# Turning six of twelve probability chunks by DMA, with a single buffer, and moving the row statistics and the normalized rows in a two-layer graph attention kernel

## The reference

```python
# layer 0
scores = where(adj > 0, x @ w0 @ inp.T, -2**32 + 1)
x = layernorm(x + softmax(scores / 0.07, axis=1) @ inp)
# layer 1
Wh = x @ W;  s1 = Wh @ a1;  s2 = Wh @ a2
e = leaky_relu(s1[:, None] + s2[None, :], 0.2)
att = softmax(where(adj > 0, e, -9e15), axis=1)
x = layernorm(x + elu(att @ Wh))
```

## Time and profile before

| what | value |
|---|---|
| median of 3 runs | 1454.98 us |
| the profiled execution's own time | 1453.21 us |
| its span, first to last instruction | 1451.4 us |
| TensorE busy | 1412.1 us, 97% |
| VectorE busy | 1256.5 us, 87% |
| GpSimd busy | 1215.0 us, 84% |
| ScalarE busy | 1070.0 us, 74% |
| packets of the main DMA queue, share of 16 engines | 73.1% |
| granted TensorE clock, mean | 0.989 |

### The profile page before, as it was taken

How to read it: one execution, slowest core, us unless ns; L and a number is a source line. 1 busy time by engine, 2 the same in 40 slices (tenths; PEclk the granted TensorE clock), 3 DMA queues, 4 the chain that set the end, 5 groups by cost and what they waited for, 6 DMA issues and landing times.

```text
span 1451.4 us, 28334 instructions
## 1 busy us (share of the span) xinstructions
PE 1412.1 (97%) x9661; PEld 1010.3 (70%) x9661; DVE 1256.5 (87%) x2129; ACT 1070.0 (74%) x2437; POOL 1215.0 (84%) x904
## 2 busy tenths in 40 slices
PE   8899999999999999999999999979999999999995
PEld 4577777777777777777777777755666666666664
DVE  6999999999999899999999999839898898979794
ACT  6788888888888888888888888868655555545453
POOL 6788888888888888888888878738999999999995
PEclk9999999999999999999999999998999999999998
DMA  8999999999999999999999999663434344434320
GB/s 265 292 270 269 262 265 257 258 275 270 270 267 263 259 264 258 273 271 271 273 258 259 262 255 274 182 138 73 102 66 111 77 102 87 102 71 105 78 58 14
DMA packets 427918, 291.38 MB, mean 201 GB/s; under 512 B 356864, under 2 KB 403200, under 8 KB 427776
## 3 DMA queue, kind: packets, MB, share of 16 engines
q1 hardware_dynamic: 427776, 289.59, 73.1%
HBM read 160.56 MB, written 40.89 MB: 139 GB/s over the span
## 4 chain that ended last, share of the span: by engine, by line
PE 94%; DVE 3%; issue 1%; ACT 1%; POOL 0%; DMA 0%; ACTq 0%; DVEq 0%; SPq 0%; POOLq 0%
PE ps L617 17%; PE ps L703 13%; PE ps L696 12%; PE ps L643 11%; PE ps L619 9%; PE ps L656 8%; PE ps L655 8%; PE ps L654 8%; PE ps L680 6%; PE ps L587 1%; PE ps L714 1%; DVE rows L969 1%; DVE neg_mask L944 1%; PE ps L580 0%; DVE pT_lo L978 0%
## 5 line engine op out<-in xcount | busy, mean ns | idle before, releaser
L826 ACT ACTIVATE rows<-rows,exp_bias 128x512 f32<-128x512 f32 x576 | 416.8, 724 | 57.0 <-DVE exp_bias L1022 57.0
L528 POOL TENSOR_TENSOR p_lo<-p,p_hi 128x1024 fp32r<-128x1024 f32 x180 | 423.7, 2394 | 22.0 <-ACT p_hi L864 11.5
L969 DVE CUSTOM_DVE_ANT_0 rows<-ps,neg_mask 128x1024 f32<-128x1024 f32 x288 | 352.1, 1223 | 80.2 <-PE ps L656 72.8
L1049 DVE SCALAR_TENSOR_TENSOR p<-ps,e_col,edgesT 128x1024 f32<-128x1024 f32 x288 | 349.7, 1275 | 53.3 <-PE ps L673 36.7
L438 POOL TENSOR_SCALAR edges<-neg_mask 128x1536 uint8<-128x1536 bf16 x190 | 307.3, 1618 | 97.0 <-DVE neg_mask L944 85.1
L864 ACT CAST p_hi<-p 128x1024 fp32r<-128x1024 f32 x180 | 185.1, 1047 | 167.0 <-DVE p L1049 164.4
L617 PE MATMUL ps<-vals,pT_hi 128*128 128x256 f16 x1536 | 295.3, 273 | 1.4 <-ACT att L805 0.9
L812 ACT CAST pT_hi<-ps 128x512 f16<-128x512 f32 x384 | 222.7, 580 | 90.6 <-PE ps L643 90.4
L480 POOL TENSOR_TENSOR inp_sb<-rows,inp_sb 128x512 f16<-128x512 f32 x192 | 281.5, 1484 | 9.6 <-ACT inp_sb L820 1.9
L619 PE MATMUL ps<-vals,pT_lo 128*128 128x128 f16 x1536 | 274.6, 219 | 0.0
L978 DVE TENSOR_TENSOR pT_lo<-ps,pT_hi 128x512 f16<-128x512 f32 x384 | 250.8, 683 | 10.6 <-ACT pT_hi L812 10.6
(11 more groups left out here) (111 smaller groups left out, 1855.9 us busy)
## 6 DMA issues: line engine op xcount, KB each, us to landing
adj_sb<-adj SPq DMA_DIRECT2D x192, 768.0 KB, 5.6
edge_rows<-edges SPq DMA_DIRECT2D x192, 192.0 KB, 4.8
xq<-x SPq DMA_DIRECT2D x48, 64.0 KB, 2.9
xr<-x SPq DMA_DIRECT2D x48, 64.0 KB, 5.6
out<-y_w SPq DMA_DIRECT2D x5, 512.0 KB, 3.7
inp_sb<-inp SPq DMA_DIRECT2D x3, 768.0 KB, 8.2
inp_sb<-inp_sb SPq DMA_TRANSPOSE x96, 4.6
edgesT<-edge_rows SPq DMA_TRANSPOSE x48, 5.3
```

Source lines behind the costliest of these rows:

```text
L528: nc.gpsimd.tensor_tensor(p1_lo[:, m % LO_SLOTS, :], p1[:, (NB * g + n) % P_SLOTS, :], p1_hi[:, m % HI_SLOTS, :].bitcast(F32), ALU.subtrac ...
L826: nc.scalar.activation(row_chunk(1 - par, c), row_chunk(1 - par, c), ACT.Exp, bias=exp_bias[:, 1 - par:2 - par], scale=EXP_SCALE, accum_ou ...
L969: nc.vector.tensor_tensor_reduce(row_pair(par, k), scores_pair(k), neg_mask_row[:, 2 * k * CHUNK:2 * (k + 1) * CHUNK], 1.0, -3.0e38, ALU.a ...
L1049: nc.vector.scalar_tensor_tensor(out=p1[:, (NB * g + n) % P_SLOTS, :], in0=ps[:, R_ROW:R_ROW + 2, :].rearrange("p b w -> p (b w)"), scalar ...
```

## The change

Six chunks instead of four go by DMA, so that six are turned by TensorE, and ATT_STEP becomes 11. `movedT` loses its second slot and is filled in two parts of three chunks, each part with a high and a low transpose of 384 KB. A part may be overwritten when the attends of the tile before have read it; the casts and subtractions of a chunk wait for the part it is in.

GpSimd's order is new: the reciprocal root is behind the first low part, the product behind the third, low parts 4 and 5 behind edges 0 and 1. It loses the normalizing and the total.

VectorE takes the row statistics of tile t - 3 at step 2 of lap t, behind the first maximum of the tile, and the normalized rows at step 4. For the last tile it also makes the two additions and the products. The total over x1 becomes eight reductions over 44 tiles in lap 48 and four more one-column products on TensorE.

```diff
-MOVED = 4
+MOVED = 6
+MOVED_PARTS = ((0, 3), (3, 6))
...
-        movedT = inp_space[:, 2 * MW:6 * MW].rearrange("p (s h b m) -> p s h b m", s=2, h=2, m=P)
+        movedT = inp_space[:, 2 * MW:4 * MW].rearrange("p (h b m) -> p h b m", h=2, m=P)
...
+        STATS_STEP, ROWS_STEP, SUMS_STEP = 2, 4, 9
+        TOTALLED, TOTAL_PARTS = NB - 4, 8
...
         def movedT_loads(tile):
-            return 32 * (tile // 2 + 1)
+            return 32 * (tile + 1)
+
+        def moved_part(i):
+            return next(k for k, (a, b) in enumerate(MOVED_PARTS) if a <= i < b)
...  SP
-                    if tile < 2:
-                        sp.wait_ge(vals_lo, MOVED * (tile + 2))
-                    after(sp, pv_done, C * (tile - 1))
-                    sp.dma_start_transpose(movedT[:, par, 0], moved_hi).then_inc(movedT_in[par], 16)
-                    sp.wait_ge(moved_lo_set, MOVED * (tile + 1))
-                    sp.dma_start_transpose(movedT[:, par, 1], moved_lo).then_inc(movedT_in[par], 16)
+                    if tile == 0:
+                        sp.wait_ge(vals_lo, 2 * MOVED)
+                    for k, (a, b) in enumerate(MOVED_PARTS):
+                        after(sp, pv_done, C * (tile - 1) + (C - MOVED) + b if tile >= 1 else 0)
+                        for half, of, ready in ((0, moved_hi, moved_hi_set), (1, moved_lo, moved_lo_set)):
+                            sp.wait_ge(ready, MOVED * tile + b)
+                            sp.dma_start_transpose(movedT[:, half, a * BPC:b * BPC, :], of[:, a * CHUNK:b * CHUNK]
+                                                   ).then_inc(movedT_in[k], 16)
...  GpSimd, one lap
                     make_edges(t, 2)
                 if moved:
                     moved_low(t - 1, 0)
+                if t >= 3:
+                    rstd_of_tile(t - 3)
+                if moved:
                     moved_low(t - 1, 1)
                 if 0 < t < NB:
                     make_edges(t, 3)
...
                 if moved:
                     moved_low(t - 1, 2)
+                if t >= 3:
+                    score_cols(t - 3)
+                if moved:
                     moved_low(t - 1, 3)
                 if ahead:
                     make_edges(t + 1, 0)
...
+                if moved:
+                    moved_low(t - 1, 4)
+                if ahead:
                     make_edges(t + 1, 1)
+                if moved:
+                    moved_low(t - 1, 5)
...
-                if ends_tile(known):
+                if 2 <= t <= NB:
...
-                    pool.wait_ge(ve_set, tile + 1)
-                    nc.gpsimd.tensor_tensor(small[:, 4:5], small[:, 3:4], consts[:, 0:1], ALU.pow).then_inc(rstd_set, 1)
-                    pool.wait_ge(rstd_set, tile + 1)
-                    nc.gpsimd.tensor_scalar(x1_all[:, tile, :], xr[:, par, :], moments[:, 0:1], small[:, 4:5], ALU.subtract,
-                                            ALU.mult).then_inc(x1_set, 1)
-                    score_cols(tile)
...  VectorE
+            def row_statistics(tile):
+                dve.wait_ge(u_set, tile + 1)
+                after(dve, x1_set, tile)
+                nc.vector.bn_stats(stats[:], xr[:, tile % 2, :]).then_inc(stats_set, 1)
+                dve.wait_ge(stats_set, tile + 1)
+                nc.vector.bn_aggr(moments[:], stats[:]).then_inc(moments_set, 1)
+                dve.wait_ge(moments_set, tile + 1)
+                nc.vector.tensor_scalar(small[:, 3:4], moments[:, 1:2], EPS, None, ALU.add).then_inc(ve_set, 1)
+
+            def normalized_rows(tile):
+                dve.wait_ge(rstd_set, tile + 1)
+                nc.vector.tensor_scalar(x1_all[:, tile, :], xr[:, tile % 2, :], moments[:, 0:1], small[:, 4:5], ALU.subtract,
+                                        ALU.mult).then_inc(x1_set, 1)
...
                 for c in range(C):
+                    if c == STATS_STEP and t >= 3:
+                        row_statistics(t - 3)
+                    if c == ROWS_STEP and t >= 3:
+                        normalized_rows(t - 3)
...
+                    if t == NB and 1 <= c <= TOTAL_PARTS:
+                        d = slice((c - 1) * P // TOTAL_PARTS, c * P // TOTAL_PARTS)
+                        dve.wait_ge(x1_set, TOTALLED)
+                        nc.vector.reduce_sum(x1_total[:, d], x1_all[:, 0:TOTALLED, d].rearrange("p n d -> p d n"),
+                                             AX_X).then_inc(total_set, 1)
```

More of the change, by code:

```diff
@@ L225, in build @@
         moved_hi_set, moved_lo_set = sem("moved_hi_set"), sem("moved_lo_set")
-        movedT_in = [sem(f"movedT_in{i}") for i in range(2)]
+        movedT_in = [sem(f"movedT_in{i}") for i in range(len(MOVED_PARTS))]
         att_out = sem("att_out")
@@ L478, in moved_low, with rstd_of_tile @@
                 if tile >= 1:
-                    pool.wait_ge(movedT_in[(tile - 1) % 2], movedT_loads(tile - 1))
+                    pool.wait_ge(movedT_in[moved_part(i)], movedT_loads(tile - 1))
                 nc.gpsimd.tensor_tensor(moved_lo[:, i * CHUNK:(i + 1) * CHUNK], row_chunk(tile % 2, i),
                                         moved_hi[:, i * CHUNK:(i + 1) * CHUNK], ALU.subtract).then_inc(moved_lo_set, 1)
+            def rstd_of_tile(tile):
+                pool.wait_ge(ve_set, tile + 1)
+                nc.gpsimd.tensor_tensor(small[:, 4:5], small[:, 3:4], consts[:, 0:1], ALU.pow).then_inc(rstd_set, 1)
             def tile_rstd(t, par, known):
@@ L717, in mean_of_wh @@
             def mean_of_wh():
-                pe.wait_ge(total_set, NB)
-                nc.tensor.matmul(ps[:, SPARE, 0:P], x1_total[:], averager[:], start=True, stop=True).then_inc(mean_turned, 1)
+                pe.wait_ge(total_set, TOTAL_PARTS)
+                nc.tensor.matmul(mean_ps, x1_total[:], averager[:, 0:1], start=True, stop=False)
+                pe.wait_ge(x1_set, NB)
+                for j in range(TOTALLED, NB):
+                    mm = nc.tensor.matmul(mean_ps, x1_all[:, j, :], averager[:, 0:1], start=False, stop=(j == NB - 1))
+                mm.then_inc(mean_turned, 1)
                 pe.wait_ge(mean_repd, 1)
-                nc.tensor.matmul(ps[:, SPARE, P:2 * P], mean_rep[:], w1_c[:, 0:P], start=True, stop=True).then_inc(mean_made, 1)
+                nc.tensor.matmul(ps[:, OUT3, P:2 * P], mean_rep[:], w1_c[:, 0:P], start=True, stop=True).then_inc(mean_made, 1)
             pe.wait_ge(masked, PAIRS * NB)
@@ L830, in tile_steps @@
                         xT_high(t + 1, 1 - par)
-                    if c == 4 and t >= 3:
+                    if c == SUMS_STEP and t >= 3:
                         score_sums(t - 3)
-                    if c == C - 1 and t == NB + 1:
-                        score_sums(t - 2)
                 if t == 0:
@@ L1005, in tile_steps @@
                                                     ALU.mult).then_inc(scaled_set, 1)
[L1006 to L1013, removed]
-                            nc.vector.tensor_scalar(small[:, 3:4], moments[:, 1:2], EPS, None, ALU.add).then_inc(ve_set, 1)
+                        if c == C - 1 and t == NB + 1:
+                            dve.wait_ge(att_out, NB)
+                            dve.wait_ge(xr_in[par], 16 * (t // 2))
+                            nc.vector.tensor_tensor(xr[:, par, :], att[:, 0:P], xr[:, par, :], ALU.add).then_inc(u1_set, 1)
+                            dve.wait_ge(u1_set, NB)
+                            nc.vector.tensor_tensor(xr[:, par, :], att[:, P:2 * P], xr[:, par, :], ALU.add).then_inc(u_set, 1)
                     if c == C - 1 and scores_of(known):
@@ L1025, in _ @@
             tiles(dve, tile_steps)
-            dve.wait_ge(s_set, NB)
+            row_statistics(NB - 1)
+            normalized_rows(NB - 1)
+            dve.wait_ge(x1_set, NB)
+            dve.wait_ge(s_set, NB - 1)
+            for k in range(2):
+                nc.vector.tensor_tensor_reduce(s_prod[:, k, :], x1_all[:, NB - 1, :], wa_rep[:, k, :], 1.0, 0.0, ALU.mult,
+                                               ALU.add, s_cols[:, k, NB - 1:NB]).then_inc(s_last_set, 1)
+            dve.wait_ge(s_last_set, 2)
             nc.vector.reduce_max(s_top[:, 0:1], s_cols[:, 0, :], AX_X).then_inc(s_part, 1)
```

22 lines of the change are left out of this document (10 added, 12 removed).

## The result

The changed kernel takes 1536.99 us (median of 4 runs, 1535.59 to 1538.53), the kernel before 1453.95 beside it (1452.54 to 1455.09): ratio 1.0575, 95% interval 1.0562 to 1.0588. The forecast was 1521 with a range of 1466 to 1562. The profiled execution took 1538.53 with a span of 1536.5, so 85.1 more than the span before.

A forecast was written before the change was run, and what follows sets the result against it. A loop through GpSimd's low parts and VectorE's first maximum and mask quarter 2 was to bound the lap at 20.92 us. 44 laps x 1.57 = 69.1, ends -0.8, on 1453.2 gave 1521 us, range 1466 to 1562.

The forecast's parts named there:

- the way over the last low part: Loop from low 5 through VectorE's first maximum and mask quarter 2 back to low 5: 20.92 us per lap.
- the ends: First laps -1.8 us, lap 47 +1.0, close -1.7, added attends and transposes +1.7: together -0.8 us.
- The closed loop through GpSimd: GpSimd's 16.81 us from edges 2 to low 5 plus VectorE's 4.11 set the lap at 20.92.
- The contention: VectorE's masks lengthen GpSimd's work beside them: 0.59, 0.78 and 0.59, together 1.96 us per lap.
- Almost the same lap, by a second way; ... so this one costs nothing more: VectorE, waiting 2.1 us for rstd in step 4, gives a 20.6 us lap; only the larger loop counts.
- VectorE's account: VectorE's lap: busy time, normalizing at 0.34, waiting for rstd 2.1 and former idling 1.77 sum to 20.6 us.
- The rule weighed in the prediction: VectorE and GpSimd share a port pair as exclusive lock; normalizing could add up to 0.34 us to GpSimd's lap.
- a large wait of L969's first maximum for GpSimd's low part, about 1 us or more per lap: Sign that VectorE's first maximum of a tile is held by the last subtraction, as the GpSimd loop requires.
- The other signs: First scores 20.9 us apart, VectorE waiting 2 for rstd, GpSimd 3 for mask quarter 2, TensorE at nine tenths or less.
- rival 4: The DMA queues bound the lap at 21.1 us, up to 22: 1529 to 1568 us in all; chance 0.10.
- Leaving the share aside: DMA time of 21.1 us per lap was kept only as a rival, since the share counts overlapping packets twice.
- The eight reductions ... stand where VectorE is half idle: Reductions of x1_all in lap 48 on VectorE, given no cost term of their own.

The follow-up runs named there:

- e2: The changed kernel with GpSimd's reciprocal root moved ahead of edges quarter 2: 1489.38 us, ratio 1.0245.
- g2: Five chunks by DMA instead of six, on a version with mask quarter 2 earlier and SP's loads and waits reordered: 1446.09 us, ratio 0.9947.
- e1: The changed kernel with the normalized rows on VectorE at step 7 instead of 4: 1578.94 us, ratio 1.0868.
- f3: As e1, with the load of the residual rows moved behind the transposes in SP's queue: 1513.66 us, ratio 1.0423.
- f4: The changed kernel with one more 512 KB transfer per lap, from adj to a scratch tensor in DRAM: 1537.93 us, ratio 1.0586.
- h1: The changed kernel with the eight reductions of lap 48 over 2 tiles instead of 44: 1535.22 us, ratio 1.0556.
- f1: The changed kernel with mask quarter 2 made at step 0, ahead of the tile's first maximum, instead of step 2: 1458.77 us, ratio 1.0033.
- f2: As f1, with the next x tile and adj quarters 0 and 1 loaded earlier in SP's queue, and GpSimd's root ahead of low part 0: 1450.62 us.
- e4: The changed kernel with four chunks by DMA instead of six, the other parts of the change kept: 1585.24 us, ratio 1.0903.
- e5: The changed kernel with the normalized rows back on GpSimd, right behind the root: 1575.3 us, ratio 1.0841.

## Why the prediction was right, and which terms were not

The direction and the range held, and so did the picture of two ways of almost one length that meet in the mask of quarter 2. Which of them counts did not: the forecast added up the way over the last low part, and the lap is set by the other. That the sum came within 16 us is in part luck, since the two lie 0.2 us apart. The 16 us (the sum itself gives 1521.5): 10.8 from the laps (44 x 0.245) and 6 from the ends (5.2 instead of -0.8), less 1.5 for the median, which lies that much below the profiled execution.

- **The closed loop through GpSimd**: right in length, but not what binds. Its part from edges 2 to the end of low 5 was to be 16.81 and is 523.33 - 506.47 = 16.86. From low 5 to the next edges 2 it is 4.30 instead of 4.11, of which 0.2 are the maximum's waiting for TensorE. But 16.86 is partly luck. The contention was taken as 1.96 for three masks; mask 3 met a waiting GpSimd, so only low parts 2 and 3 paid, 1.74 + 1.88 - 2 x 1.16 = 1.30. In the place of the rest stands a wait of 1.11 for mask 3, and rstd, product and low parts were together 0.40 shorter than summed.
- **"Almost the same lap, by a second way; ... so this one costs nothing more"**: this is the step that failed. VectorE's account was put at 20.6 with the normalizing at 0.34. The wait ahead of it was right, 2.00 for 2.1. The operation took 1.17, beyond the upper bound of 0.80, because it begins 0.07 us after GpSimd's low part 1 (509.65) and ends with it: 0.83 too small, and 20.6 + 0.83 = 21.4 (21.16 measured, on the way walked above). Away from a low part it took 0.38 (e2), with GpSimd idle 0.33 (the last tiles). The rule weighed in the prediction (the Trainium skill, SBUF — State Buffer, section Who interferes with whom) speaks of exactly this lock, and the traces agree: wherever the operation began inside an instruction of GpSimd, it ended 0.08 or 0.09 us after that instruction (1.17 us here, 0.92 in g2, 1.49 beside edges in e1). That is less than the 0.33 that it takes alone, so which part of it was held up the traces don't tell. But I had applied it in one direction only, as what VectorE takes from GpSimd. What GpSimd takes from VectorE was the larger.
- **Sign to look for**: "a large wait of L969's first maximum for GpSimd's low part, about 1 us or more per lap" was wrong for this kernel: 4.3 us in all. The low part ends at 523.33, 0.23 before the maximum, which then waits for TensorE. The loop was nearly tied and hidden; f3 and e2 bring it into the open (waits of 68.5 and 80.3 us). The other signs held: laps of 21.2 for 20.9, 3.35 + 1.11 of waiting for masks on GpSimd for some 3, TensorE at nine tenths, hardly a wait for a landing.
- **DMA** (rival 4): f4 rules it out at this lap. Leaving the share aside was right; that it counts overlapping packets twice was argued, and no run shows it.
- **The ends**: att to s_top is 3.45 for 3.7, right. "The eight reductions ... stand where VectorE is half idle" was wrong: at 1.35 each they are some 10.7 us, and cost 1.8 (h1). With the two attends and the last transposes they make 4.1 us of the seam, where 1.7 was taken. The first laps gave -0.8 for -1.8, the last +1.1 for +1.0; the uneven laps' 1.4 were in no term. Nor was the second stage's 1.4, which is no cost of its four more products: it takes 476.7 us here and 475.2 in the kernel before, but 475.1 to 475.3 in e2, f1 and f2, where it is the same code as here. What makes it differ stays open.

## What to carry to other kernels

When work moves between engines, close the loops before adding up busy times: follow each engine's first instruction of a lap back through what it waits for until the same instruction comes again, and look for a stretch that all loops share. One instruction moved out of that stretch was worth 78 us here, more than any other single edit. And a load in one in-order queue that waits for a result (the residual rows) ties that result to everything behind it: move the consumer and the queue becomes the next loop.

## What the runs showed of the hardware

- A small f32 tensor_scalar of 128x128 takes 0.33 to 0.35 us on VectorE alone. Begun inside an instruction of GpSimd it ended 0.08 us after that one: 1.17 beside a subtraction (the changed kernel, 45 of 48 times 1.17 or 1.18), 0.92 when begun 0.3 us into one (g2), 1.49 beside edges (e1, 12 times), 0.38 near the end of edges (e2).
- A DMA share above 1.0, up to 1.13 with 296 GB/s, went with hardly a wait for a landing in the changed kernel; adding 8% of bytes (f4) brought such waits, none of them on the path, and cost nothing. In f2 a share of 1.10 to 1.13 went with 67.2 us of waiting for transposes.
- A reduction over a strided view, 128x704 f32 to 128x16, took 1.35 us, 0.18 for 128x32.
- TensorE's granted clock was at its upper level (1.00, 2.4 GHz) throughout the even laps of e4, at 88 to 90% busy, and in the changed kernel but for two falls, at 88 to 91%. In e1 and e5, whose laps are uneven at 85 to 90% busy, it fell to its lower level 18 times each (0.97 in the mean of the laps). Laps with a fall took 0.8 us more than the others in the changed kernel at the least, and 3.4 in f1 at the most. Why it falls in one kernel and not in the other stays open.
